# Turning the input tiles with VectorE instead of TensorE, and adding the identity to the weight, in a kernel of two batched LoRA layers

## The reference

```python
# layer 0: base weight, bias and adapter of rank 16
x = x + (einsum('bsd,od->bso', x, base_weight) + base_bias
         + einsum('bsr,bor->bso', einsum('bsd,brd->bsr', x, A0[ids0]), B0[ids0]))
# layer 1: adapter of rank 16 alone, factor 1
x = x + einsum('bnr,bor->bno', einsum('bni,bri->bnr', x, B1[ids1]), A1[ids1])
```

## Time and profile before

| | |
|---|---|
| median of 3 runs | 121.97 us (121.28 to 122.36) |
| span of the profiled execution | 120.5 us, from its first to its last instruction |
| busy, share of the span | PE 86%, PEld 82%, DVE 69%, ACT 40%, POOL 57% |
| mean granted TensorE clock | 0.983 of full speed |
| DMA | 19.39 MB, mean 161 GB/s |

### The profile page before, as it was taken

How to read it: one execution, slowest core, us unless ns; L and a number is a source line. 1 busy time by engine, 2 the same in 40 slices (tenths; PEclk the granted TensorE clock), 3 DMA queues, 4 the chain that set the end, 5 groups by cost and what they waited for, 6 DMA issues and landing times.

```text
span 120.5 us, 2716 instructions
## 1 busy us (share of the span) xinstructions
PE 104.1 (86%) x726; PEld 98.6 (82%) x726; DVE 82.7 (69%) x246; ACT 48.0 (40%) x128; POOL 68.5 (57%) x93
## 2 busy tenths in 40 slices
PE   6996939739689299999999999999999999999990
PEld 6986929739587298989898988989898988989890
DVE  0047677544899976786878787687868778687552
ACT  4039538153453033333536343343536343343300
POOL 6200684027775717686858668685857768670800
PEclk9999999999999859999999999999999999999998
DMA  4999899913622714453737374563736354560213
GB/s 82 370 272 259 272 348 213 258 69 110 182 61 99 212 48 131 152 175 108 197 102 254 54 244 111 173 180 104 213 93 248 87 210 125 158 197 0 93 41 133
DMA packets 11766, 19.39 MB, mean 161 GB/s; under 512 B 1360, under 2 KB 5840, under 8 KB 11600
## 3 DMA queue, kind: packets, MB, share of 16 engines
q1 hardware_dynamic: 10480, 14.04, 38.0%
q0 software_dynamic: 1280, 5.28, 16.0%
HBM read 13.47 MB, written 5.84 MB: 160 GB/s over the span
## 4 chain that ended last, share of the span: by engine, by line
PE 47%; DVE 23%; DMA 16%; SPq 5%; issue 4%; ACT 1%; DVEq 1%; POOL 0%; POOLq 0%
PE psum L444 32%; DVE u_own L689 15%; DMA ids<-in_itok_B 9%; PE psum L483 9%; PE psum L474 7%; DMA by_rank<-row_ends 4%; DVE u_blocks L686 4%; DMA gathered_rows<-by_rank,rows_now_even 3%; DVE g_sel L678 2%; SPq L199 1%; SPq L194 1%; SPq L190 1%; DVE xt L627 1%; DVE wd L668 1%; SPq L197 1%
## 5 line engine op out<-in xcount | busy, mean ns | idle before, releaser
L444 PE MATMUL psum<-wd,xt 128*128 128x256 f32 (+1 forms) x384 | 67.1, 318 | 0.2 <-DVE y L702 0.2
L444 PEld LDWEIGHTS psum<-wd,xt 128*128 128x128 f32 x384 | 57.6, 193 | 0.7 <-DVE y L702 0.4
L292 POOL TENSOR_TENSOR xb<-x_in,bias_all 128x512 f32<-128x512 f32 x16 | 21.0, 1314 | 9.1 <-DVE y L702 9.0
L549 ACT ACTIVATE up_rows<-gathered_rows 128x512 fp32r<-128x512 f32 x16 | 10.1, 634 | 32.2 <-PE psum L444 26.4
L285 POOL TENSOR_TENSOR up_rows<-gathered_rows,up_rows 128x512 fp32r<-128x512 f32 x16 | 21.2, 1327 | 0.2 <-ACT up_rows L549 0.2
L689 DVE SCALAR_TENSOR_TENSOR u_own<-u_blocks,bb_sel,batch_mask 128x128 f32<-128x128 f32 x16 | 18.3, 1144 | 0.6
L702 DVE TENSOR_TENSOR y<-psum,xb 128x512 f32<-128x512 f32 x15 | 10.4, 691 | 9.7 <-PE psum L483 9.0
L549 ACT ACTIVATE wd<-table_rounded 128x128 fp32r x64 | 14.6, 298 | 3.5 <-issue 3.5
L483 PE MATMUL psum<-up_rows,u_sel 128*128 128x256 f32 x96 | 13.9, 281 | 0.0
L474 PE MATMUL psum<-u_own,g_sel 128*128 128x128 f32 x32 | 8.1, 336 | 6.7 <-DVE u_own L689 6.7
L474 PEld LDWEIGHTS psum<-u_own,g_sel 128*128 128x128 f32 x32 | 5.0, 195 | 10.7 <-DVE u_own L689 10.7
(11 more groups left out here) (67 smaller groups left out, 84.8 us busy)
## 6 DMA issues: line engine op xcount, KB each, us to landing
x_in<-in_x SPq DMA_DIRECT2D x16, 256.0 KB
out<-y SPq DMA_DIRECT2D x15, 256.0 KB, 2.9
bw_rows<-in_L_cond_lora_B_w SPq DMA_DIRECT2D x1, 1024.0 KB, 4.9
w_rows<-in_L_cond_base_weight SPq DMA_DIRECT2D x2, 512.0 KB, 8.7
a_rows<-in_L_cond_lora_A_w SPq DMA_DIRECT2D x1, 1024.0 KB, 12.3
by_rank<-bw_by_rank SPq DMA_DIRECT2D x4, 256.0 KB
by_rank<-row_ends SPq DMA_DIRECT2D x1, 330.0 KB
b_rows<-in_L_cond_B SPq DMA_DIRECT2D x1, 256.0 KB, 5.0
```

The source lines that it names most:

```text
L292: nc.gpsimd.tensor_tensor(out=xb[:, slot, :], in0=x_in[:, slot, :], in1=bias_all[:, :], op=ALU.add).then_inc(xb_ready, 1)
L444: last = nc.tensor.matmul(psum[:, 2 * slot + half, start:end], xt[:, slot, c, x_part, :], wd[:, w_part, c, col:col + end - start], start=( ...
L549: return nc.scalar.activation(dst, src, ACT.Copy)
```

## The change

- x is loaded by four DMAs per block in place of one. DMA g brings columns 128 g to 128 g + 127 of all four batches to partitions 32 g to 32 g + 31: 32 rows (s) by 4 batches by 128 columns, in pieces of 512 bytes.
- One VectorE instruction (x_turn) transposes the 32x32 squares of a block into the PSUM bank XT, reading each fourth column (i c, with c innermost, so that chunk c holds columns 4 i + c). TensorE's transposes of x go. To match, w and lora_a are read with the same step of four columns (chunk) by their transposes and by C1.
- GpSimd adds the identity to the four diagonal 128x128 pieces of w_rows at the start (w_plus). All fills of w now wait for both halves of w and for the four adds; they stay where they were, ahead of and behind G.
- GpSimd's add_bias goes with xb; finish adds bias_all. VectorE's c1_sum goes, since C1 holds b1 through the identity.
- u_blocks moves from SBUF to PSUM bank 6.
- The selection for layer 1 moves from VectorE to ScalarE, behind that of layer 0. On ScalarE u_high(k - 1) moves ahead of xt_high(k + 1). On VectorE x_turn(k + 1) stands where xt_low(k + 1) was, and xt_low(k + 1) moves behind u_split(k - 1).
- Loads of x wait for xt_filled alone. In the start-up TensorE no longer waits for x block 1.

The core of the diff:

```diff
@@ -47,7 +47,7 @@
-    x_blocks = x.rearrange("(k a) s d -> k (a s) d", a=NB)
+    x_squares_of = x.rearrange("(k b) s (g e) -> k g s b e", b=NB, g=P // S)
@@ -101,18 +100,17 @@
-        u_blocks = sb("u_blocks", [P, P])
...
-        xb = sb("xb", [P, 2, D])
...
-        U, EDGE_U, XT = 4, 5, 7
+        U, EDGE_U, U_BLOCKS, XT = 4, 5, 6, 7
+        u_blocks = banks[U_BLOCKS][:, 0:P]
@@ -173,6 +171,10 @@
+        def chunk(rows_of, c):
...
+            return rows_of.rearrange("p (m c) -> p c m", c=C)[:, c, :]
@@ -182,6 +184,12 @@
+            def load_squares(k, slot):
...
+                for g in range(P // S):
+                    sp.dma_start(x_squares[g * S:(g + 1) * S, slot, :, :],
+                                 x_squares_of[k, g, :, :, :]).then_inc(x_loaded[slot], 16)
@@ -285,19 +292,18 @@
-            def add_bias(k, pair, slot, free=True):
-                pool.wait_ge(x_loaded[slot], pair * 16 + 16)
-                if free:
-                    pool.wait_ge(y_ready, k - 1)
-                nc.gpsimd.tensor_tensor(out=xb[:, slot, :], in0=x_in[:, slot, :], in1=bias_all[:, :],
-                                        op=ALU.add).then_inc(xb_ready, 1)
...
-            def step(k, slot, next_pair):
+            def step(k, slot):
...
-                add_bias(k + 1, next_pair, 1 - slot)
...
+            pool.wait_ge(ident_ready, 1)
+            for half in range(2):
+                pool.wait_ge(w_in[half], 16)
+                for oc in range(half * C // 2, (half + 1) * C // 2):
+                    diagonal = w_rows[:, oc, oc * P:(oc + 1) * P]
+                    nc.gpsimd.tensor_tensor(out=diagonal, in0=diagonal, in1=ident[:, :],
+                                            op=ALU.add).then_inc(w_plus, 1)
@@ -383,13 +385,14 @@
-                    if c % 2 == 0:
-                        pe.wait_ge(w_in[c // 2], 16)
...
-                                                   w_rows[:, oc, c * P:(c + 1) * P], ident[:, :])
+                                                   chunk(w_rows[:, oc, :], c), ident[:, :])
...
+            pe.wait_ge(w_in[0], 16)
+            pe.wait_ge(w_in[1], 16)
+            pe.wait_ge(w_plus, C)
@@ -400,31 +403,21 @@
-            def transpose_x(pair, slot):
...
-                pe.wait_ge(x_loaded[slot], pair * 16 + 16)
-                for c in range(C):
-                    last = nc.tensor.transpose(banks[XT][:, c * P:(c + 1) * P], x_in[:, slot, c * P:(c + 1) * P],
-                                               ident[:, :])
-                last.then_inc(xt_filled, 1)
...
-            transpose_x(0, 0)
...
-                                               a_rows[:, g, c * P:(c + 1) * P], ident[:, :])
+                                               chunk(a_rows[:, g, :], c), ident[:, :])
...
-                    cols = slice((h * C // 2 + c) * P, (h * C // 2 + c + 1) * P)
...
-                        last = nc.tensor.matmul(bank(C1_FILL[h])[:, c * P:(c + 1) * P], w_rows[:, oc, cols],
-                                                b1_cols[:, oc, :], start=(oc == 0), stop=(oc == C - 1))
+                        last = nc.tensor.matmul(bank(C1_FILL[h])[:, c * P:(c + 1) * P],
+                                                chunk(w_rows[:, oc, :], h * C // 2 + c), b1_cols[:, oc, :], start=(oc == 0), stop=(oc == C - 1))
@@ -571,12 +566,14 @@
-            def select(k, slot, n0, free=True):
+            def select(k, slot, free=True):
...
-                for b in range(NB):
-                    last = copy(selected(slot, b, L0), table0_rounded[:, bass.ds(n0[b], 1), :, :, :])
-                last.then_inc(sel0_ready, 1)
+                for layer, ready, table in ((L0, sel0_ready, table0_rounded), (L1, sel1_ready, table1_rounded)):
+                    n = adapters_of(act, k, layer)
+                    for b in range(NB):
+                        last = copy(selected(slot, b, layer), table[:, bass.ds(n[b], 1), :, :, :])
+                    last.then_inc(ready, 1)
@@ -592,25 +589,23 @@
+                u_high(k - 1)
...
-                u_high(k - 1)
-                select(k + 1, 1 - slot, adapters_of(act, k + 1, L0))
+                select(k + 1, 1 - slot)
...
-            first_n0 = [adapters_of(act, s, L0) for s in range(2)]
...
-                act.wait_ge(c1_summed, h + 1)
+                act.wait_ge(filled, C1_FILL[h] + 1)
...
-                copy(table1_rounded[:, :, 0, chunks, :],
-                     c1_sum[:, chunks, :].rearrange("p c (n r) -> p n c r", r=R)).then_inc(act_drained, 1)
-            wait_drained(act, A_FILL + 3)
-            select(0, 0, first_n0[0], free=False)
+                copy(table1_rounded[:, :, 0, chunks, :], c1_by_adapter(h)).then_inc(act_drained, 1)
+            wait_drained(act, C1_FILL[1])
+            select(0, 0, free=False)
...
-            select(1, 1, first_n0[1], free=False)
+            select(1, 1, free=False)
@@ -656,17 +651,19 @@
+            def x_turn(k, slot, loads, free=True):
...
+                if free:
+                    dve.wait_ge(xt_lo_ready, k)
+                dve.wait_ge(x_loaded[slot], loads * 16 * (P // S))
+                nc.vector.transpose(out=banks[XT].rearrange("p (c b s) -> p b c s", c=C, b=NB),
+                                    in_=x_squares[:, slot, :, :].rearrange("p b (i c) -> p b c i", c=C),
+                                    ).then_inc(xt_filled, 1)
...
-            def select(k, slot, n1, free=True):
-                if free:
-                    dve.wait_ge(u_filled, k - 1)
-                for b in range(NB):
-                    last = nc.vector.tensor_copy(selected(slot, b, L1), table1_rounded[:, bass.ds(n1[b], 1), :, :, :])
-                last.then_inc(sel1_ready, 1)
@@ -683,10 +680,10 @@
-                nc.vector.transpose(out=u_blocks[:, :], in_=source).then_inc(u_blocks_ready, 1)
+                nc.vector.transpose(out=u_blocks, in_=source).then_inc(u_blocks_ready, 1)
...
-                nc.vector.scalar_tensor_tensor(out=u_own[:, :], in0=u_blocks[:, :], scalar=bb_sel[:, slot, :],
+                nc.vector.scalar_tensor_tensor(out=u_own[:, :], in0=u_blocks, scalar=bb_sel[:, slot, :],
@@ -696,29 +693,29 @@
-                dve.wait_ge(xb_ready, k + 1)
...
-                                        in1=xb[:, slot, :].rearrange("p (h n) -> p h n", h=2),
+                                        in1=bias_all[:, :].rearrange("p (h n) -> p h n", h=2),
...
-                xt_low(k + 1, 1 - slot)
+                x_turn(k + 1, 1 - slot, next_pair + 1)
...
+                xt_low(k + 1, 1 - slot)
...
-                select(k + 1, 1 - slot, n1)
...
+            x_turn(0, 0, 1, free=False)
@@ -728,19 +725,13 @@
-                dve.wait_ge(filled, C1_FILL[h] + 1)
-                nc.vector.tensor_tensor(out=c1_sum[:, chunks, :],
-                                        in0=bank(C1_FILL[h])[:, 0:D // 2].rearrange("p (c m) -> p c m", c=C // 2),
-                                        in1=b1_cols[:, chunks, :], op=ALU.add).then_inc(c1_summed, 1)
-                dve.wait_ge(c1_summed, h + 1)
...
-                low(table1_rounded[:, :, 1, chunks, :], c1_sum[:, chunks, :].rearrange("p c (n r) -> p n c r", r=R),
+                low(table1_rounded[:, :, 1, chunks, :], c1_by_adapter(h),
...
-            wait_drained(dve, C1_FILL[1])
-            select(0, 0, first_n1[0], free=False)
+            x_turn(1, 1, 1)
...
-            select(1, 1, first_n1[1], free=False)
...
+            dve.wait_ge(bias_all_in, 16)
```

More of the change, by code:

```diff
@@ L68, in two_lora_layers @@
         bias_all = sb("bias_all", [P, D])
-        x_in = sb("x_in", [P, 2, D])
+        x_squares = sb("x_squares", [P, 2, NB, P])
         ident = sb("ident", [P, P])
@@ L148, in two_lora_layers @@
         dve_drained = sem("dve_drained")
-        c1_summed = sem("c1_summed")
+        w_plus = sem("w_plus")
         bias_b1_step, bias_b1_ready = sem("bias_b1_step"), sem("bias_b1_ready")
@@ L161, in two_lora_layers @@
         rows_now_ready, gather_issued = sem("rows_now_ready"), sem("gather_issued")
-        y_ready, xb_ready = sem("y_ready"), sem("xb_ready")
+        y_ready = sem("y_ready")
         FILL_BANKS = 7
@@ L195, in _ @@
                              ids_of.rearrange("(a k) -> a k", a=1).to_broadcast([P, B])).then_inc(ids_all_in, 16)
-            sp.dma_start(x_in[:, 0, :], x_blocks[0, :, :]).then_inc(x_loaded[0], 16)
+            load_squares(0, 0)
             sp.dma_start(a_rows[:, :, :], lora_a.rearrange("(g n) r d -> (n r) g d", g=C)).then_inc(a_in, 16)
@@ L213, in _ @@
             sp.dma_start(by_rank_dram.rearrange("(g p) c -> p g c", p=P)[:, :, D:ROW], row_ends[:, :, :]).then_inc(table_stored, 16)
-            sp.dma_start(x_in[:, 1, :], x_blocks[1, :, :]).then_inc(x_loaded[1], 16)
+            load_squares(1, 1)
             def load(k, slot):
                 sp.wait_ge(xt_filled, k - 1)
-                sp.wait_ge(xb_ready, k - 1)
-                sp.dma_start(x_in[:, slot, :], x_blocks[k, :, :]).then_inc(x_loaded[slot], 16)
```

(18 more changed lines are left out.)

3 lines of the change are left out of this document (removed).

## The result

The kernel after takes 118.08 us, the median of 4 runs (116.41 to 120.83), against 121.65 for the kernel before on the same chip (4 runs, 121.28 to 122.36): a ratio of 0.958 with an interval of 0.951 to 0.965. The profiled execution took 116.41 us with a span of 114.5; before it was 120.5. I forecast 119.9, and steps of 5.15 us with the g_sel copies held up. The time is inside the range, but the kernel inside is another one than I described: the steps take 4.72 (4.69 and 4.75 in turn), and the start costs more than I gave it.

What follows compares the result with a forecast made beforehand. TensorE bounds the kernel, with 0.43 us of each step empty because GpSimd's bias add holds u_own. Terms +0.7 + 0.65 - 2.9 - 0.5 = -2.05 take the span from 120.5 to 118.4, plus 1.5 gives 119.9 us; range 113.5 to 123.8.

Steps and rivals of the forecast that it cites:

- TensorE's step, 4.63: Steady step: TensorE's own work without the four x transposes and the empty 0.43 us, 4.63 us.
- u_own 0.35, x_turn 1.1, not held: Steady step on VectorE: u_own falls from 1.10 to 0.35 us, the new x_turn takes 1.1, neither held by GpSimd.
- So what is held is an instruction with all its operands and its output in SBUF: VectorE beside GpSimd: only all-SBUF instructions are held; u_own, reading u_blocks from PSUM, takes 0.35 us for 1.10.
- And the indirect DMA holds as the arithmetic does: Steady step: GpSimd's indirect DMA holds the g_sel copies, y comes late, a step takes 5.15 us, 2.9 saved over twelve.
- rival A: Steady step: the indirect DMA doesn't hold the g_sel copies, 8.3 us saved over twelve steps, 113.7 us; chance 22%.
- Start-up: Before the steady steps: w fills start at 13.1, base product of block 1 at 34.6, block 3 at 47.6, +0.7 us.
- The C1 term: Start-up on TensorE: C1's 32 stepped loads at 0.157 each take 5.0 us for 3.74, bounds 3.7 and 5.9.
- the memory rule: Start-up: reads slow when each goes to a new 16-byte line; if 16-byte steps read as dense, 2.3 us shorter.
- The clock loss of 0.65: Wait before block 3: TensorE idles some 3 us; half of a 1.3 us lower-clock loss is added, +0.65.
- Rival C: Start-up costs more than counted: C1 at 5.9, both clock losses whole, 122.1 us; chance 18%.
- Rival B: Steady step: x_turn becomes the bound and the kernel gets slower, 124.7 us, or 131 if 2.1 and held; chance 15%.
- D: Loads of x: the squares arrive late, deciding when landing takes over 3.4 us; counted within the slower and costlier-start rivals.

Runs made afterwards that it cites:

- the pair of runs with the add: Kernel after plus one unused GpSimd 128x512 add behind each indirect DMA of blocks 3 to 14: queued at once 130.11 us, waiting for y 118.55 us.
- after_w_copied: Kernel after, with VectorE copying w plus identity into chunk order so that C1 reads dense weights: 115.17 us, ratio 0.949 to the kernel before.
- after_g_first: Kernel after, with G computed ahead of all w fills while TensorE waits for the diagonal adds: 116.82 us, ratio 0.955 to the kernel before.
- after_add_later: Kernel after, with an unused GpSimd 128x512 add behind each indirect DMA of blocks 3 to 14, waiting for y: 118.55 us, ratio 0.969.

## Why the prediction was right in the sign and wrong in the size

By its own steps:

- **TensorE's step, 4.63: right.** 4.72 measured, with TensorE busy throughout.
- **u_own 0.35, x_turn 1.1, not held: right.** 0.351 and 1.118, and neither is held. The 1.1 was a choice between bounds of 0.72 and 2.3, so that its closeness is partly luck: no run has the transpose without the step.
- **"So what is held is an instruction with all its operands and its output in SBUF": right**, and it was worth more than I saw. I put it to use only for u_own within the whole change and never asked what moving u_blocks alone would do. It gives 7.5 us of span by itself (120.5 to 113.0).
- **"And the indirect DMA holds as the arithmetic does": the step that failed.** From it came P = 5.15, copies over 1 us and -2.9 for twelve steps; measured 4.72, copies of 0.17, and -7.1. The overlap that I predicted is there (the DMA at 76.28 in the copies of 76.01), but without the effect. Both cases in the earlier trace rows had arithmetic ready behind the DMA: behind the one of 33.72 stood the subtract of 34.74, and behind the one of 37.84 stood two instructions, which the timeline of before shows on GpSimd without a gap:

```profile
38.86 1.27 POOL L292 TENSOR_TENSOR xb<-x_in,bias_all 128x512 f32<-128x512 f32 x1
40.08 1.26 POOL L285 TENSOR_TENSOR up_rows<-gathered_rows,up_rows 128x512 fp32r<-128x512 f32 x1
```

They end at 41.34, and the u_own of 38.14 at 41.50. I read the 0.69 us beside the DMA as the DMA's doing; the pair of runs with the add shows that it was the queue's. In a steady step the next subtract on GpSimd must first wait for ScalarE's part (1.24 us idle before it), so nothing is ready, and the copies pass. The Trainium skill, SBUF — State Buffer, "Who interferes with whom", says that a two-input VectorE operation does not stop descriptor generation. In this kernel the indirect DMA with nothing ready behind it does not stop a copy either, but for 0.2 us in its last third; with arithmetic ready behind it a copy of 0.17 that starts 0.39 to 0.45 into it takes 1.65 us or more. Had I priced rival A by the question of what stands ready behind the DMA, it would have had more than its 22%: its 4.70 is, but for 0.02, the step that was measured.
- **Start-up: mis-sized.** The w fills began at 12.78 (13.1 forecast) at 0.52 of the clock: right. The C1 term was 5.0 with 5.9 as the upper bound and measured 7.6. I carried the price of a transpose's stepped load over to a matmul's; the measured prices are 0.127 and 0.236, and neither is the 0.157 that I took from the earlier trace rows. That figure was no price of a step either. It is the mean of sixteen loads of which, in the trace of before, the first six come 0.213 us apart and the others 0.112. In the kernel after the same sixteen, at the same step of 64 bytes, take 2.00 us in place of 2.51:

```profile
5.76 2.00 PEld L376 LDWEIGHTS psum<-ident,bw_rows 128*128 128x128 f32 x16
```

So the earlier trace rows doesn't show that reads with a step of 64 bytes lose speed, as I wrote under the memory rule, and the earlier trace rows has no dense copy beside it. The step of 16 bytes of this change is not read as if it were dense: C1 takes twice its time. The base product of block 1 came at 34.98 all the same (34.6 forecast): C1 began at 21.8, 1.6 before its place in my sum (0.3 from the earlier w fills, the rest from fills at 0.127 and not 0.157 a load), and what lies between its end and block 1 took 5.5 in place of 6.2. Then the landing of the gather of block 3: 3.7 forecast, 5.4 measured (41.50 to 46.9). Block 3 started at 48.62, 1.0 later than the 47.6 of the sum, +1.66 against before in place of +0.7. The clock loss of 0.65 that I added in the wait before block 3 did not come in the profiled execution; the profiles of after_w_copied, after_g_first and after_add_later have a slice at 0.5 there.
- **Tail: right,** -0.6 for -0.5.

Together: forecast +0.7 + 0.65 - 2.9 - 0.5 = -2.05; measured +1.7 + 0 - 7.1 - 0.6 = -6.0. Of the 4 us between the two the failed step makes 4.2; that the start came out 1.0 worse and the clock loss 0.65 better nearly cancel. Rival A's sum of -8.25 misses by 2.25, half in the start (+0.55 for +1.7) and half in the steps (-8.3 for -7.1: one step of 5.43, 4.72 for 4.70, and the twelve of before taking 5.37 and not 5.39). Rival C, the costly start, took place as well as A, beside it, not instead; I had given them as alternatives. Rival B did not come, and D in one block alone: x_turn waited 0.45 us for its squares there, and that step was 0.7 longer.

Shown by runs: that the queue behind the indirect DMA holds the copies; that u_own in PSUM is freed, and that without the bias add it is freed where GpSimd is idle; that the dense C1 gives 3.9 us back in its own matmuls. Argued only: that the lower clock behind the 4.4 us wait costs its share of the 4.4 us of later start, since after_g_first took most of the wait away and the clock fell all the same, behind the next one; and why the gather of block 3 landed in 5.4 us, though the four x loads, 41.83 on, share the DMA engines with it. Not tried: reading w and x in runs of 32 neighbouring columns in place of every fourth, which might make C1's reads denser.

## What to carry to other kernels

When one instruction takes three times its own arithmetic beside GpSimd, ask first what it costs to move one of its operands to PSUM; here that one line gave 6%, and the rest of a much larger change gave part of it back. For each instruction that may be held, look not only at what GpSimd runs but at what stands ready behind it. And price a folded-in constant by what must now wait for it: the identity in the weight let four short matmuls and a bias add per step go, and put both halves of the weight and four adds ahead of the first fill, which sixteen blocks did not earn back: on one chip the whole change took 117.73 us and its one line alone 115.25.

## What the runs showed that I had not expected

- A GpSimd add that is ready behind an indirect DMA holds VectorE's SBUF copies while the DMA is still being issued: 1.65 to 1.71 us for a copy of 0.17 that starts 0.39 to 0.45 into it, where the same DMA with nothing behind it costs none or, in its last third, 0.2.
- An operand in PSUM takes the instruction out of this altogether: u_own with one tensor input in PSUM took 0.35 us beside the same indirect DMA and the add ready behind it (38.21), against 3.36 with both in SBUF.
- A stationary operand read at every fourth float costs a float32 matmul twice the time (C1 3.74 to 7.62 us for 32) and a transpose almost nothing (0.108 to 0.127 each).
- The transpose of 128x512 on VectorE from SBUF with that step into PSUM takes 1.118 us, between 1.103 and 1.136 in all sixteen.
